# Top-k attention with its units cut another way: 32 queries of four heads in place of 128 queries of one

## The reference, cut to what matters

```python
scores = einsum('bhqd,bhkd->bhqk', q, k) / sqrt(16)
scores = where(causal, -inf, scores)               # keys behind the query's position are masked
vals, idx = top_k(scores, 32)
attn = softmax(only the 32 largest of each row, the rest -inf)
out = einsum('bhqk,bhkd->bhqd', attn, v) @ Wo.T + bo
```

## Time and profile before

| what | value |
|---|---|
| median of 3 runs | 2365.05 us (2362.78 to 2369.48) |
| the profiled execution: span from first to last instruction | 2362.0 us |
| what lies around the span, taken as the median less it | 3 us |
| VectorE busy | 1641.8 us, 70% |
| TensorE busy, with a granted clock of 0.50 in `attend_top` | 1451.2 us, 61% |
| ScalarE busy | 953.0 us, 40% |
| GpSimd busy | 465.1 us, 20% |

### The profile page before, as it was taken

One profiled execution on the slowest core, in us unless ns is written; L12 is line 12 of the kernel. 1 busy time (PEld: TensorE's weight loads), 2 busy tenths in 40 slices (PEclk: granted clock), 3 DMA queues, 4 the chain that ended last, 5 costly groups with the idle time before them and its releaser, 6 DMA issues. The chain is left out here.

```text
span 2362.0 us, 37247 instructions
## 1 busy us (share of the span) xinstructions
PE 1451.2 (61%) x8100; PEld 794.3 (34%) x8101; DVE 1641.8 (70%) x4922; ACT 953.0 (40%) x1997; POOL 465.1 (20%) x856
## 2 busy tenths in 40 slices
PE   6489989678887079991734444444444444446982
PEld 3122235334445046660422222222222222223661
DVE  3478856667765211112649999999999999996456
ACT  2156653235552022220325554555544545543330
POOL 4100002200000400005323333333333333330000
PEclk9699999879997589996765555555555555557995
DMA  4472311533305111112250000000000000001001
GB/s 151 149 243 75 83 41 37 149 101 75 83 22 220 65 38 45 46 45 82 82 148 19 19 19 19 19 19 19 19 19 19 19 19 19 19 1 45 0 0 37
DMA packets 98268, 137.64 MB, mean 58 GB/s; under 512 B 11284, under 2 KB 77724, under 8 KB 97312
## 3 DMA queue, kind: packets, MB, share of 16 engines
q1 hardware_dynamic: 94816, 127.37, 18.3%
q0 software_dynamic: 3264, 8.41, 1.1%
HBM read 82.49 MB, written 53.76 MB: 58 GB/s over the span
## 5 line engine op out<-in xcount | busy, mean ns | idle before, releaser
L1074 DVE MATCH_REPLACE8 top_left<-top_largest,top_left 128x129 f32<-128x129 f32 (+3 forms) x768 | 361.1, 478 | 1.0 <-issue 0.6
L1072 DVE MAX8 top_largest<-top_left 128x8 f32<-128x129 f32 (+3 forms) x768 | 338.5, 482 | 1.6 <-DVE top_largest L1072 1.0
L898 PE MATMUL top_ps_pt<-ident,top_prob 128*128 128x128 f32 x640 | 193.9, 439 | 198.7 <-POOL top_prob L1004 195.8
L979 ACT ACTIVATE top_e_left<-top_left,top_neg_max 128x129 f32<-128x129 f32 (+3 forms) x256 | 134.4, 561 | 312.0 <-DVE top_left L1074 305.8
L906 PE MATMUL top_ps_pv<-top_prob_t,top_vs 128*32 128x128 f32 x1280 | 82.9, 421 | 269.0 <-ACT top_prob_t L954 269.0
L1004 POOL TENSOR_TENSOR top_prob<-top_e_all,top_e_left 128x129 f32<-128x129 f32 (+3 forms) x256 | 202.5, 812 | 10.2 <-ACT top_e_left L979 3.3
L898 PEld LDWEIGHTS top_ps_pt<-ident,top_prob 128*128 128x128 f32 x640 | 107.6, 211 | 287.2 <-POOL top_prob L1004 272.3
L665 DVE TENSOR_REDUCE tok_rowmax<-tok_ps_s 128x1 f32<-128x512 f32 x256 | 167.1, 689 | 44.8 <-PE tok_ps_s L508 42.3
L1562 DVE TENSOR_TENSOR moe_hid<-moe_act_gate,moe_ps_h 128x512 f32<-128x512 f32 x39 | 26.8, 688 | 220.3 <-ACT moe_act_gate L1523 220.3
L906 PEld LDWEIGHTS top_ps_pv<-top_prob_t,top_vs 128*32 128x32 f32 x1280 | 50.7, 163 | 297.7 <-ACT top_prob_t L954 294.5
L665 DVE TENSOR_REDUCE rot_rowmax<-rot_ps_s 128x1 f32<-128x128 f32 (+3 forms) x256 | 115.8, 488 | 45.1 <-PE rot_ps_s L511 41.1
(11 more groups left out here) (327 smaller groups left out, 3098.9 us busy)
## 6 DMA issues: line engine op xcount, KB each, us to landing
moe_w<-in_moe_w SPq DMA_DIRECT2D x3, 4096.0 KB, 24.0
moe_xs<-zeros SPq DMA_DIRECT2D x1, 5120.0 KB, 18.7
last_xs<-zeros SPq DMA_DIRECT2D x1, 5120.0 KB, 31.7
moe_rows<-moe_xs SPq DMA_DIRECT2D x40, 128.0 KB
moe_ys<-moe_y SPq DMA_DIRECT2D x38, 128.0 KB
v_rows<-tok_va SPq DMA_DIRECT2D x16, 256.0 KB, 4.0
tok_vs<-v_rows SPq DMA_DIRECT2D x16, 256.0 KB
v_rows<-rot_va SPq DMA_DIRECT2D x16, 256.0 KB, 3.4
```

What stands on the lines that cost most here:

```text
L898: mm = pe.transpose(ps_t[:, i, ch * P:ch * P + P], prob[:, qt % 2, u % HG, 1 + ch * P:1 + ch * P + P], c.ident[:, :])
L979: act.activation(e_left[:, i, 0:w], left[:, j, 0:w], ACT.Exp, bias=neg_max[:, j:j + 1]).then_inc(left_ok, 1)
L1072: ins = dve.max(largest[:, at, j // 2, :], src)
L1074: ins = dve.match_replace(left[:, at, 0:w], largest[:, at, j // 2, :], src, TAKEN)
```

## The change

Units are cut as **32 queries of all four heads of the group**: a unit `U` is row block `j = U % 16` of step `s`, its 128 rows are four heads of 32 queries, and its width is 33 + 32 j columns, so that all queries of a unit see nearly the same keys. Keys stand by position, the class token among them. Each head's scores go to 32 partitions of PSUM by matmuls of their own (one for the keys before the block, one for the block's own 32 keys, in which 32 more rows of `qs` and `ks` carry the mask). There is no `raw` copy: VectorE's first MAX8 and ScalarE's exponential both read PSUM. The later rounds work on exponentials: `e8` are those of the eight largest, MATCH_REPLACE8 puts 0 in the chosen places, and `prob` is `e - left`, in place. The values are stored to DRAM by position too (`v_by_position`), 128 positions a chunk, and the position that is left over at the end of each query tile comes as a `tail`: one column turned by itself and one matmul of one row for each head. The class token has no path of its own any more. Denominators and scaling are done image by image, the scaling on GpSimd. All loops are written out.

TensorE runs `values` for four units, which were one head each before and now are 32 queries of all heads; the loop over heads is now outside, that over chunks inside.

```diff
 def project
+    by_position = cls and not rope
...
-                for g in range(G):
-                    sp.dma_start(c.vd[b, g], va[:, b * NQ:b * NQ + NQ, g * HG:g * HG + HG, :].rearrange(
-                        "p n h s -> p n (h s)")).then_inc(v_out, 16)
+                if by_position:
+                    rows = va[:, b * NQ:b * NQ + NQ, :, :].rearrange("p n (g h) s -> p n g (h s)", g=G)
+                    sp.dma_start(c.vp[b, :, 0:1, 1:, :].rearrange("g p n w -> p n g w"), rows[P - 1:P]
+                                 ).then_inc(v_out, 16)
+                    for g in range(G):
+                        sp.dma_start(c.vp[b, g, 1:, 0:NQ, :], rows[0:P - 1, :, g, :]).then_inc(v_out, 16)
...
+            if by_position:
+                sp.wait_ge(vc_ok, 1)
+                sp.dma_start(c.vp[:, :, 0, 0, :], vc[:, :, :].rearrange("b (g h) s -> b g (h s)", g=G)
+                             ).then_inc(v_out, 16)
...
 def attend_top, TensorE
+            def scores(U):
...
+                if U >= SLOTS:
+                    pe.wait_ge(e_ok, U - SLOTS + 1)
+                for h in range(HG):
...
+                    pe.matmul(ps[lanes, base:base + own - first], q[0:PARTS * HD, h, mine],
+                              k[0:PARTS * HD, h, first:own], start=True, stop=True)
+                    mm = pe.matmul(ps[lanes, base + own - first:base + own - first + QS], q[:, h, mine],
+                                   k[:, h, own:own + QS], start=True, stop=True)
+                mm.then_inc(s_mm, 1)
...
+            def values(n):
...
+                pe.wait_ge(t_out, 4 * n + 4)
+                pe.wait_ge(tail_ok, n + 1)
+                for h in range(HG):
+                    lanes = slice(QS * h, QS * h + QS)
+                    for ch in range(J + 1):
+                        pe.matmul(ps_pv[lanes, :], v[:, ch, lanes], prob_t[:, n % 2, ch, h, :],
+                                  start=ch == 0, stop=False)
+                    mm = pe.matmul(ps_pv[lanes, P - QS:P], v[0:1, J + 1, lanes], tail_t[:, n % 2, lanes],
+                                   start=False, stop=True)
                 mm.then_inc(pv_mm, 1)
+                pe.wait_ge(pv_out, n + 1)
+                pe.transpose(ps_back, pv_rows[:, :], c.ident[:, :]).then_inc(bt_mm, 1)
+            def use(U):
+                turn(U)
+                if U % 4 == 3:
+                    values(U // 4)
...
+            for U in range(4, units, 2):
+                scores(U)
+                if U >= 6:
+                    use(U - 6)
+                    use(U - 5)
+                scores(U + 1)
...
 ScalarE
+            def expo(U):
+                if U >= KEPT:
+                    act.wait_ge(t_mm, U - KEPT + 1)
+                act.wait_ge(neg_ok, U + 1)
+                act.activation(e[:, U % KEPT, 0:keys(U)], row(U), ACT.Exp, bias=neg_max[:, U % 4:U % 4 + 1]
+                               ).then_inc(e_ok, 1)
+                act.activation(e8[:, U % 4, :], raw8[:, U % 4, :], ACT.Exp, bias=neg_max[:, U % 4:U % 4 + 1]
+                               ).then_inc(e8_ok, 1)
...
+            for U in range(2, units, 2):
+                expo(U)
+                expo(U + 1)
+                if U >= 4:
+                    use(U - 4)
+                    use(U - 3)
...
 GpSimd
+            for U in range(2, units, 2):
+                if U >= 4:
+                    subtract(U - 4)
+                    subtract(U - 3)
+                negate(U)
+                negate(U + 1)
+                if U + 2 < units:
+                    pad(U + 2)
+                    pad(U + 3)
+                if U % (units // B) == 8 and U > 8:
+                    scale(U // (units // B) - 1)
...
 VectorE
+            def largest(U):
+                dve.wait_ge(s_mm, U + 1)
+                dve.max(raw8[:, U % 4, :], row(U)).then_inc(max_ok, 1)
+            def take_first(U):
+                w = keys(U)
+                dve.wait_ge(e_ok, U + 1)
+                dve.wait_ge(e8_ok, U + 1)
+                if U >= 4:
+                    dve.wait_ge(prob_ok, U - 3)
+                dve.match_replace(left[:, U % 4, 0:w], e8[:, U % 4, :], e[:, U % KEPT, 0:w], 0.0).then_inc(pick, 1)
...
+            for U in range(0, units, 2):
+                pair = (U, U + 1)
+                for u in pair:
+                    take_first(u)
+                for u in pair:
+                    find(u, 1)
+                if U + 2 < units:
+                    largest(U + 2)
+                    largest(U + 3)
+                for step in (2, 4):
+                    for u in pair:
+                        take(u, step)
+                    for u in pair:
+                        find(u, step + 1)
+                for u in pair:
+                    take(u, 6)
```

More of the change, by code:

```diff
@@ L913, in use @@
-            def use(b, g, k):
-                turn_pair(b, g, k)
-                if 2 * k % HG == HG - 2:
-                    values(b, g, 2 * k // HG)
-            def step(b, g, before, more):
-                for k, last in with_before(b, g, before):
-                    ahead(score_pair, b, g, k, more)
-                    if last:
-                        use(*last)
-            for b in range(B):
-                mm = pe.matmul(ps_s[:, b // 2, b % 2 * S:b % 2 * S + D], c.pick_cls[:, b, :], c.vcls[:, :],
-                               start=True, stop=True)
@@ L934, in _ @@
+            def use(U):
+                turn(U)
+                if U % 4 == 3:
+                    values(U // 4)
+            pe.wait_ge(masks_ok, 2 + 2 * HG)
+            for U in range(4):
+                scores(U)
+            for U in range(4, units, 2):
+                scores(U)
+                if U >= 6:
+                    use(U - 6)
+                    use(U - 5)
+                scores(U + 1)
+            for U in range(units - 6, units):
+                use(U)
         @block.scalar
@@ L1027, in step @@
-            def step(b, g, before, more):
-                for k, last in with_before(b, g, before):
-                    for i in range(2):
-                        u, j = 2 * k + i, 2 * (k % 2) + i
-                        pool.wait_ge(pick, picked(b, g, k, 0, i))
-                        pool.wait_ge(left_ok, unit(b, g, u + 1))
-                        pool.nop(nofuse=True)
-                        pool.tensor_scalar(neg_max[:, j:j + 1], largest[:, j, 0, 0:1], -1.0, None, ALU.mult
-                                           ).then_inc(neg_ok, 1)
-                    if last:
-                        if last[2] % 2 == 0 and (before or k > 1):
-                            finish(*((last[0], last[1], last[2] // 2 - 1) if last[2] else
-                                     (last[0], last[1] - 1, NQ - 1)))
-                        use(*last)
@@ L1043, in _, with negate @@
[L1043 to L1048 removed]
+            def negate(U):
+                pool.wait_ge(max_ok, U + 1)
+                if U >= 4:
+                    pool.wait_ge(e8_ok, U - 3)
+                pool.tensor_scalar(neg_max[:, U % 4:U % 4 + 1], raw8[:, U % 4, 0:1], -1.0, None, ALU.mult
+                                   ).then_inc(neg_ok, 1)
@@ new lines, in _ @@
+            negate(1)
+            for U in range(2, units, 2):
+                if U >= 4:
+                    subtract(U - 4)
[7 more added lines that the diff above has]
+                    scale(U // (units // B) - 1)
+            for U in range(units - 4, units):
+                subtract(U)
@@ L1050, in _ @@
+            scale(B - 1)
         @block.vector
         def _(dve):
[L1052 to L1075 removed]
@@ new lines, in take, with denominators @@
+            def take(U, step):
+                w = keys(U)
+                dve.wait_ge(pick, U // 2 * 12 + 2 * (step - 1) + 1 + U % 2)
+                ins = dve.match_replace(left[:, U % 4, 0:w], next8[:, U % 2, step // 2 - 1, :], left[:, U % 4, 0:w], 0.0)
+                ins.then_inc(left_ok if step == 6 else pick, 1)
+            def denominators(b):
+                dve.wait_ge(back_ok, NQ * G * (b + 1))
+                tiles = slice(b * NQ, b * NQ + NQ)
+                dve.reciprocal(rden[:, tiles, :], ctx[:, tiles, :, HD]).then_inc(den_ok, 1)
@@ new lines, in _ @@
+            dve.tensor_copy(c.ctx[0:B, NT, :], c.vcls[:, :]).then_inc(masks_ok, 1)
+            largest(0)
+            largest(1)
+            for U in range(0, units, 2):
[14 more added lines that the diff above has]
+                    take(u, 6)
+                if U % (units // B) == 6 and U > 6:
+                    denominators(U // (units // B) - 1)
```

380 lines of the change are left out of this document (156 added, 224 removed).

## The result

The changed kernel takes 2634.88 us (median of 4 runs, 2633.70 to 2636.09), the one before 2363.91 (4 runs, 2362.74 to 2369.48): a ratio of 1.1141 [1.1128, 1.1154]. It is 11% slower. The forecast was 2318 us and a range of 2256 to 2412, so it was wrong in sign and size.

A forecast was written before the change was run, and what follows sets the result against it. VectorE alone was taken to set the time. Terms -102.4 - 6.2 + 2 + 60 + 1.9 + 0.5 + 1.5 - 4.5 = -47 took the span from 2362.0 to 2315, so 2318 us measured; 8-in-10 range 2256 to 2412.

The forecast's parts named there:

- VectorE's work: VectorE in `attend_top`: narrower units -102.4 us, no loop jumps -6.2, stalls of narrow operations +2.
- Zero for the PSUM source: VectorE's first MAX8 of a unit reading PSUM instead of SBUF: taken to cost 0 extra.
- Projection: SP issues four v stores at 0.94 us each ...; now five and one more: +1.9: End of the projection, SP's queue: two more store issues for an image, priced at 0.94 us each, +1.9 us.
- I take the overlapped price, as the nearest row: TensorE's `values` of four chunks: four heads assumed side by side, 32 passes in 1.93 us as in the old trace.
- The values run head after head: Rival on TensorE: next head waits for ten passes, four-chunk `values` about 7.2 us, 2437 us in all; chance 0.19.
- a two-pass tail: TensorE's `values`: each head's chunks take eight passes plus a two-pass tail before the next head; no separate price.
- strict FIFO, no reordering: Skill's rule for TensorE matmuls, cited on the head-after-head rival: by it that rival holds; the old order spoke against it.
- The chain of the change of step: Waits across engines when wide units give way to narrow: 3.6 us before the sixth unit, 4.0 in all, 15 times, +60.
- The start: Start of `attend_top`: no raw copy (-0.5), but first pick waits for negate, table load and exponentials; +1.5 us in all.
- The end: After the last match in `attend_top`: 15.4 us before, 10.9 after, -4.5 us.
- The 0.4 us for `e8`: VectorE's wait for `e8` at a change of step, before the third unit's match: 0.4 us of the 4.0.
- Theory D: From the experiments: TensorE hands out matmuls as written; each column group holds one running, three waiting; a full group blocks later ones.

The follow-up runs named there:

- e7: e6 with values in DRAM position after position, so each projection store takes a whole tile of 128 rows: 2253.17 us, ratio 0.9520 to the kernel before.
- e1: The changed kernel with each 127-row v store of the projection cut into 112 and 15 rows: 2460.02 us, ratio 1.0404 to the kernel before.
- e4: The kernel before, old layout kept, with its projection v stores cut into 127 rows and 1 row: 2546.73 us, ratio 1.0769.
- e2: e1 with the one-row tail matmuls behind all other matmuls of `values`, heads still outside and chunks inside: 2339.44 us, ratio 0.9898 to the kernel before.
- e3: e1 with chunks outside and heads inside in `values`, tails last: 2311.76 us, ratio 0.9783 to the kernel before.
- e9: e1, order of heads and tails kept, with the tail matmul reading 128 rows, all but the first zero: 2356.41 us, ratio 0.9945 to the kernel before.
- e8: e1 with the heads of `values` in pairs (0 and 1, then 2 and 3), tails last: 2323.15 us, ratio 0.9820 to the kernel before.
- e5: e3 with both units' scores ahead of the older units' `use` on TensorE: 2284.50 us, ratio 0.9649 to the kernel before.
- e6: e5 with the turn back and ScalarE's copies around it one pair later: 2257.48 us, ratio 0.9532 to the kernel before.
- e10: e7 with GpSimd's negates of a pair ahead of its subtractions of an older pair: 2263.92 us, ratio 0.9559 to the kernel before.

## Why the prediction was wrong, by its own steps

**VectorE's work was right.** The forecast was -102.4 - 6.2 + 2 = -106.6 us on the 894.2 of the earlier trace rows. In e7, where VectorE's waits in the stage come to 3.8 us, the first MAX8 is at 1225.97 and the last match ends at 2013.08: 787.1 us, so -107.1. That it meets the forecast to half a microsecond is in part luck: it still holds the wait for `e8` (below, 0.5 us a step), which the forecast had booked with the stalls, so the work itself came out some 7 us better. In the changed kernel it is 985.8 - 192.4 = 793.4, so -100.8, some microseconds in smaller waits aside. Zero for the PSUM source was right: 437 ns mean from PSUM beside 433 from SBUF over the same widths. The estimate that the prediction made from the page "VectorE: DVE Perf Modes" of the Trainium skill, section "The TRN2 errata", was 16.5 us in 256 operations, 64 ns each. The rows show 4.

**The step that failed first: "Projection: SP issues four v stores at 0.94 us each ...; now five and one more: +1.9".** It priced a store by what SP spent on one of 128 rows and counted stores. A store of 127 rows took 11.3 to 12 us. With the whole edge at +1.9 + 0.5 forecast and +173.7 measured, this term alone turns the sign. E1 took 175 us of it away, e4 put 182 on the old kernel by the number of rows alone.
The Trainium skill has it, on the page "DMA: Bandwidth & Descriptors", section "Why a DMA increments its semaphore by 16 and not by 1": a transfer is spread over the largest number of DMA engines, up to 16, that divides the size of the slowest dimension on both its sides, so 127 rows fall on one. The trace agrees: 22 GB/s and a share of 0.07 of the 16 engines for 127 rows, 222 GB/s and 0.73 for 128, and cutting into 112 and 15 ends it. The rule spoke against the change, and the prediction didn't weigh it.

**The second: "I take the overlapped price, as the nearest row".** The 2.1 us for `values` of four chunks measured 6.5 to 7.1 us, and the stalls behind `values` 192 us in place of 54 (15 of 3.6). The rival *The values run head after head* gave 7.2 us, and its 2437 us is near what the kernel takes once the stores are mended (2460). That nearness is partly luck. Its 7.2 us is for a clock of 0.50, at which the heads are 2.09 us apart and four would take 8.4; only the rise of the clock brings them down to 7. And it had no wait at the tenth unit, where 1.8 us were measured behind only two passes a head. Its mechanism, how far TensorE looks ahead, carries the smaller part: e2 to e3 is 28 us. The larger, e1 to e9 104 us and e1 to e2 121 us, is the tail of one row, which the prediction had as "a two-pass tail" with nothing to its price.
The Trainium skill, page "TensorEngine Tiling (Array Packing)", section "Key Properties", says that a change of tiling mode, not of the tile alone, drains TensorE. E9 agrees, with 104 us for 64 times four tails, 0.4 us each. That a matmul of one row among those of 128 is such a change is this case's reading; the section doesn't say it.
The prediction's rule from "TensorE: Matmul & The Clock Gate" of the Trainium skill, Part 3, "strict FIFO, no reordering", doesn't hold here: in e9 two passes of the second head start before the first head's tail, which is written ahead of them.

**The chain of the change of step was right.** From the starts of MAX8s, the mean stall at the sixth unit (over thirteen steps; e9 from its waits):

| kernel | order of `values` | passes of four chunks | stall, sixth unit | others in a step |
|---|---|---|---|---|
| after, e1 | head, its tail, next head | 6.5 to 7.1 us | 7.7 us | 5.2 us |
| e2 | heads, then tails | 3.9 to 4.5 (last 4.34) | 5.5 | 0 |
| e9 | as e1, tail of 128 rows | 4.4 to 5.6 | 6.0 | 0.2 |
| e8 | pairs, then tails | 2.79 | 4.4 | 0 |
| e3 | chunks outside, then tails | 1.93 | 3.6 | 0 |
| e5 | as e3, scores first | 1.93 | 0 (1.9 at the fifth unit's match) | 0 |

From e3 to e8 and e2 the stall grows by nearly as much as `values` does (0.8 and 1.9 us for 0.86 and 2.41). With the two terms put right, by e1's stores and by e3's order, which also moves the tails behind all heads, the forecast of 2318 us meets 2311.8.

**Small terms.** The start: 14.1 us from the first issue to the first MAX8, as before; the prediction put TensorE's 9.99 us there down to the loads, while their row has "issue", and no run shows which. The end: -4.5 forecast, -0.4 measured, since it holds the long `values` once (VectorE's wait there is 12.0 us, and 7.4 in e3). The 0.4 us for `e8` was right, 0.5 in every step but the first (3.13 us between the fourth unit's MAX8 and the fifth's, 2.63 in the first step). The 5.2 us behind the stage were not looked into.

**What stays open.** That SP's issues last 11 to 12 us from the second slow store on is seen, but not what holds them. Theory D's "three waiting" rests on four orders of one shape; other shapes weren't tried. Of the tail's shape only one row and 128 were tried.

## What to carry to other kernels

Before a transfer is priced by its bytes or by the one beside it, look at how many rows it has: cutting one row off a tile of 128 made a store of 256 KB last 11 to 12 us. With a cut in 112 and 15 the stage starts 4.9 us later than before the change (e1), with a layout that lets all 128 go 0.7 us (e7). Keep TensorE's small matmuls of another height behind a block of full ones, or pad them with zeros, and write matmuls for different column groups in turn. When a stall is taken away, ask what stands behind it in every list: here the order of scores gave half of its gain to ScalarE's copies until these moved too (e5, e6), and an instruction moved ahead of ready work can cost more than it wins (e10).

The best kernel found, e7, keeps the change's units and takes 2253.17 us, 4.8% below the kernel before.

## What the runs showed of the hardware that was not expected

- Matmuls of different column groups overtake each other, by what looks like a fixed depth: 20, 12 and 8 starts (4.49, 2.79 and 1.93 us at a clock of 0.50) for the same 32 passes in three orders.
- A one-row matmul of 32 columns between heads, 0.24 to 0.31 us by its record, costs 104 us in 256 times by its shape alone (e1 to e9).
- A DMA store of 127 rows runs at 22 GB/s, and from the second on SP spends 10.9 to 12.3 us on the issue, where one of 128 rows takes 0.84 us (3.37 for four, e7).
